# Cross-attention and a mixture-of-experts layer: operand rows spread over all partitions, one normalisation folded into the weights, raw operands kept apart, new orders

## What is computed

```python
h = x + xattn(layernorm(x), ctx, Wq, bq, Wk, bk, Wv, bv, Wo, bo)
out = h + ffn(layernorm(h), G, gate_w, up_w, down_w, lora_A, lora_B)

# xattn: 16 heads of 16
scores = jnp.einsum('bhsd,bhtd->bhst', Q, K) * scale
attn = jax.nn.softmax(scores, axis=-1)
ctx = jnp.einsum('bhst,bhtd->bhsd', attn, V)
# ffn: 8 experts, 2 of them weighted
scores = jax.nn.softmax(jnp.einsum('bsh,he->bse', x, G), axis=-1)
value, indices = jax.lax.top_k(scores, TOPK)
gate = jax.nn.silu(jnp.einsum('bsh,efh->bsef', x, gate_w))
up = jnp.einsum('bsh,efh->bsef', x, up_w)
out = jnp.einsum('bsef,bse,ehf->bsh', gate * up, w, down_w)
lr = jnp.einsum('bsh,erh->bser', x, lora_A)
out = out + LORA_SCALE * jnp.einsum('bser,bse,ehr->bsh', lr, w, lora_B)
```

## Time and profile before

| | us |
|---|---|
| median of 3 runs | 154.72 (154.31 to 155.24) |
| span of the profiled execution, first to last instruction | 150.3 |
| TensorE busy | 123.6 (82%) |
| VectorE busy | 93.0 (62%) |
| ScalarE busy | 68.7 (46%) |
| GpSimd busy | 49.3 (33%) |

### The profile page before, as it was taken

How to read it: one execution, slowest core, us unless ns; L and a number is a source line. 1 busy time by engine, 2 the same in 40 slices (tenths; PEclk the granted TensorE clock), 3 DMA queues, 4 the chain that set the end, 5 groups by cost and what they waited for, 6 DMA issues and landing times.

```text
span 150.3 us, 2628 instructions
## 1 busy us (share of the span) xinstructions
PE 123.6 (82%) x936; PEld 94.6 (63%) x936; DVE 93.0 (62%) x189; ACT 68.7 (46%) x116; POOL 49.3 (33%) x76
## 2 busy tenths in 40 slices
PE   5998661928998586499998499998999999999980
PEld 5996451928886463366574258755667578788760
DVE  4451606006498969238799569999859535866801
ACT  3116540241164243658937431989596731415110
POOL 7978602064052109800007030253500750250000
PEclk9999996595599879659999869999999999999999
DMA  4931699999999992000999100000000002002022
GB/s 133 258 133 38 144 128 187 122 156 134 171 240 142 146 255 40 2 4 4 156 122 124 20 0 4 0 4 2 7 0 0 0 4 70 0 0 74 0 74 70
DMA packets 9181, 11.92 MB, mean 79 GB/s; under 512 B 1296, under 2 KB 5712, under 8 KB 9168
## 3 DMA queue, kind: packets, MB, share of 16 engines
q1 hardware_dynamic: 8128, 10.56, 39.8%
q10 hardware_dynamic: 1040, 1.18, 4.6%
HBM read 4.34 MB, written 1.05 MB: 36 GB/s over the span
## 4 chain that ended last, share of the span: by engine, by line
PE 61%; DMA 13%; issue 7%; DVE 5%; SPq 4%; POOL 4%; ACT 3%; ACTq 0%; POOLq 0%; DVEq 0%
PE unit L719 23%; DMA qstack<-q_lo 8%; PE unit L832 7%; PE unit L800 7%; PE unit L726 5%; DMA kstack<-k_lo 5%; PE unit L819 5%; SPq L311 4%; PE unit L841 4%; PE unit L739 3%; PE unit L875 2%; POOL wf_lo L450 2%; PE unit L877 2%; PE unit L876 2%; DVE rowmax L644 1%
## 5 line engine op out<-in xcount | busy, mean ns | idle before, releaser
L644 DVE TENSOR_REDUCE rowmax<-unit 128x4 f32<-128x1024 f32 x32 | 37.7, 1214 | 18.6 <-PE unit L800 18.6
L549 ACT ACTIVATE probs<-unit 128x1024 f32<-128x1024 f32 x32 | 31.5, 1024 | 15.2 <-PE unit L819 9.8
L800 PE MATMUL unit<-kstack,qstack 48*128 48x256 f32 x128 | 16.0, 358 | 9.5 <-DMA qstack<-q_lo 3.3
L800 PEld LDWEIGHTS unit<-kstack,qstack 48*128 48x128 f32 x128 | 11.2, 227 | 15.7 <-issue 9.8
L426 POOL TENSOR_SCALAR vare<-mv 128x2 f32<-128x2 f32 x8 | 1.8, 223 | 52.2 <-DVE mv L591 52.1
L832 PE MATMUL unit<-probs,vaug 128*32 128x256 f32 x256 | 17.9, 409 | 0.0
L819 PE MATMUL unit<-qstack,kstack 49*128 49x256 f32 x128 | 13.7, 318 | 1.4 <-DVE rowmax L644 0.9
L819 PEld LDWEIGHTS unit<-qstack,kstack 49*128 49x128 f32 x128 | 10.1, 202 | 5.8 <-issue 2.9
L588 DVE BATCH_NORM_STATS2 stats<-xs 128x6 f32<-128x256 f32 x16 | 6.0, 418 | 9.9 <-DMA xs<-x 9.7
L832 PEld LDWEIGHTS unit<-probs,vaug 128*32 128x32 f32 x256 | 7.3, 115 | 6.3 <-issue 2.5
L719 PE MATMUL unit<-wf_hi,xT_hi 128*128 128x256 f32 (+1 forms) x32 | 9.4, 374 | 0.5 <-POOL xT_lo L441 0.5
(11 more groups left out here) (108 smaller groups left out, 241.6 us busy)
## 6 DMA issues: line engine op xcount, KB each, us to landing
kstack<-k_hi SPq DMA_DIRECT2D x16, 128.0 KB, 9.1
qstack<-q_hi SPq DMA_DIRECT2D x12, 128.0 KB, 8.2
xs<-x SPq DMA_DIRECT2D x4, 256.0 KB, 6.4
kstack<-k_lo SPq DMA_DIRECT2D x8, 128.0 KB, 10.8
out<-res SPq DMA_DIRECT2D x4, 256.0 KB, 2.2
probs<-wattn SPq DMA_DIRECT2D x3, 256.0 KB, 6.8
cT<-ctxT SPq DMA_DIRECT2D x3, 256.0 KB, 7.0
qstack<-q_lo SPq DMA_DIRECT2D x6, 128.0 KB, 7.0
```

The costliest lines, as they stand in the source:

```text
L549: act.activation(probs[:, n % NPAIR], unit[PAIR[name, n] // 2][:], ACT.Exp, scale=SCALE).then_inc(exp_done, 1)
L644: dve.tensor_reduce(rowmax[:, b % 2, :, :, i].rearrange("p t j -> p j t"), unit[PAIR[name, n] // 2][:], AX.X, ALU.max)\
L800: ins = pe.matmul(dst[:, j, t], qs[rows, i, t * P:(t + 1) * P], ks[rows, i], start=True, stop=True)
```

## The change

Six things change, and nearly every stage is written anew around them.

- **Rows of the stacks.** The part g of a stack now lies in the partitions g, g+4, g+8 and so on, 32 of them, and one transfer of 256 KB fills them from all 128 partitions of a part. A batch has six such transfers in place of twelve. The fourth row of each four, 3, 7, 11 and so on, is a filler: -1 in `kstack`, 0 in `qstack`, where the maxima then go into the partitions 63 and 127 with one transfer. The matmuls run over all 64 rows of a half. Fillers of stack 0 come from memsets, those of stacks 1 and 2 from four transfers of 256 KB (`fillk`, `fillq`) out of a small tile `edge`; batch 3 has a small one.
- **Raw operands.** `wk`, `wq`, `wv`, `wf` and all four contexts have tiles of their own. `probs` holds six pairs (four before).
- **Projections.** `k`, `q` and `v` of all batches are products of whole words. The splits of `wattn`, of the contexts and of the first transposes are gone (the new `wkh`, `chi` and their like stand in the code and in no order). `glu` stays of parts for batches 0 to 2 and is of whole words for batch 3; `low` is of whole words.
- **Second norm.** The weights of the second layer lose their column means once (`mean`, `mlow` on TensorE, `wfc`, `wlc` on VectorE). The rows go into the transpose as they are, and the reciprocal deviation is applied behind: as the scale of the tanh, in the routing and in the weights of the experts.
- **Smaller ones.** Ten warm-up matmuls (24 before). The tiles `xo`, `res` and `lw` are gone: the sums go back into `xs` and `low`. The ranks of the gates take four instructions in place of five.
- **Orders.** All five rows of `ORDERS` are new. SyncE issues all loads but those of ScalarE ahead of the first stack transfer, and all stack transfers.

The core of the diff:

```diff
-WHOLE = {("k", 0), ("q", 0), ("v", 0)}
+KV_PARTS = ()
+GLU_PARTS = (0, 1, 2)
+LOW_BY_VECTOR = (0,)
+NORM_BY_VECTOR = (0,)
...
     "sync": """
...
-        x:0 wv x:1 wk c:1 wq c:2 khi:0 x:2 c:3 klo:0 khi:1 qhi:1 x:3 klo:1 outs qlo:1 khi:2 qhi:2 wf klo:2
...
+        x:0 wk wv x:1 fillq:2 fillk:1 x:2 c:3 wo x:3 c:2 wd ks0:0 ks1:0 qs0:0 qs1:0 fillq:1 ks0:1 fillk:2 ks1:1
...
-        def stack_rows(engine, stack, parts, g, j, stacked):
-            lo = HALF * j + HD * g
-            engine.dma_start(stack[lo:lo + HD].bitcast(F32).rearrange("r (q k) t -> r q (k t)", k=KT),
-                             parts[HALF * j:HALF * (j + 1)].bitcast(F32).rearrange("p k t -> p (k t)")).then_inc(stacked, 16)
...
+        def part_rows(stack, g):
+            return stack[g:P:4].bitcast(F32).rearrange("i (q k) t -> i q (k t)", k=KT)
+
+        def parts_of(tile):
+            return tile.bitcast(F32).rearrange("p k t -> p (k t)")
...
+                    for g in (0, 1):
+                        sp.dma_start(part_rows(kstack[b], g), parts_of(k_hi[:, b % 2])).then_inc(k_stacked[b], 16)
...
+                        sp.dma_start(qstack[b][3:P:4].bitcast(F32),
+                                     edge[:, 1].bitcast(F32).unsqueeze(1).to_broadcast([QUAD, PAIRS, S]))\
+                            .then_inc(q_stacked[b], 16)
...
+                    wait_stacked(sp, "q", b)
+                    sp.dma_start(qstack[b][HALF - 1:P:HALF].bitcast(F32),
+                                 mT[:, b % 2].bitcast(F32)).then_inc(m_stacked[b], 16)
...
+                if name == "mean":
+                    wait(pe, "ones")
+                    pe.wait_ge(wf_in, 16)
+                    for k in range(KT):
+                        ins = pe.matmul(dst.rearrange("p o f -> p (o f)"), mean[:], wf[:, k, 0:2 * EF],
+                                        start=(k == 0), stop=(k == KT - 1))
```

More of the change, by code:

```diff
@@ L22 @@
 QUAD = 32
-GROUPS = HEADS // 4
 BLK = S // QUAD
@@ L42 @@
+GLU_PARTS = (0, 1, 2)
+LOW_BY_VECTOR = (0,)
+NORM_BY_VECTOR = (0,)
+WEIGHED_BY_GPSIMD = (0, 1, 2)
 ORDERS = {
     "tensor": """
[L44 to L56, removed]
+        xT:0@0 k:0@1 q:0@0 k:1@2 mean@1 xT:2@0 xT:1@3 bias@4 max:0.0@6 max:0.1@2 q:1@5 max:0.2@0 max:0.3@2 k:2@4
+        max:0.4@6 max:0.5@2 v:0@5 max:0.6@0 max:0.7@6 q:2@4 max:1.0@2 max:1.1@6 k:3@5 max:1.2@0 mrow:0@4 v:2@2
@@ L57 @@
     """,
     "scalar": """
[L59 to L63, removed]
+        c:0 wq biases obias c:1 wf xTE:0 khi:0 qhi:0 n1:1 n1:2 khi:1 kw:1 xTE:1 xTE:2 qhi:1 qw:1 n1:3 khi:2 kw:2
@@ new lines, in _ @@
+                if name == "wlc":
+                    wait(dve, "mlow")
+                    for k in range(KT):
+                        ins = dve.tensor_tensor(wf[:, k, 2 * EF:], wf[:, k, 2 * EF:], work[BANK["mlow", 0, 0]][:, 0, 0:LOW],
+                                                ALU.subtract)
+                    ins.then_inc(done["wlc"], 1)
+                if name == "mx":
+                    wait(dve, "max", b, i)
+                    if b >= 2 and i == 0:
+                        wait(dve, "mrow", b - 2)
+                    dve.tensor_reduce(rowmax[:, b % 2, :, :, i].rearrange("p t j -> p j t"), unit[BANK["max", b, i] // 2][:],
+                                      AX.X, ALU.max).then_inc(done["mx"], 1)
@@ L713, in _ @@
+                if name == "wl":
+                    weigh_low(dve, done, b)
+                if name == "wh":
+                    weigh_hidden(dve, done, b)
+                if name == "res":
+                    wait(dve, "down", b)
+                    dve.tensor_tensor(xs[:, b], work[BANK["down", b, 0]], xs[:, b], ALU.add).then_inc(done["res"], 1)
         @block.tensor
         def _(pe):
-            def product(dst, left, right, terms=((0, 0), (0, 1), (1, 0))):
+            done = raised["tensor"]
@@ L789, in _ @@
+                if name == "mlow":
+                    wait(pe, "ones")
+                    pe.wait_ge(wf_in, 16)
+                    for k in range(KT):
+                        ins = pe.matmul(dst[:, 0, 0:LOW], mean[:], wf[:, k, 2 * EF:], start=(k == 0), stop=(k == KT - 1))
+                    ins.then_inc(done["mlow"], 1)
                 if name == "max":
-                    n = PAIRS * b + i
                     if i == 0:
-                        wait_stacked(pe, k_stacked, b)
-                        wait_stacked(pe, q_stacked, b)
```

1101 lines of the change are left out of this document (543 added, 558 removed).

## The result

The changed kernel takes **128.68 us** (median, 128.62 to 128.92), beside 154.84 us (154.31 to 155.24) for the kernel before on the same chip: a ratio of 0.838, interval 0.831 to 0.845. The prediction said 142.0 us in a range of 134 to 153. Medians are over all executions, a ratio is over the undisturbed ones of both kernels, so the two can differ by up to a per cent.

What follows compares the result with a forecast made beforehand. Full DMA engines at half rate bound the early part, TensorE the part behind 85 us. Span: 26.3 + 100.8 + 3.1 + 3 + 4.4 = 137.6, plus 4.4 to the median: 142.0 us, range 134 to 153.

Steps and rivals of the forecast that it cites:

- The rate of the transfers: Stack transfers spread over all 128 partitions: taken at 250 GB/s, between 109 for narrow copies and 273 for loads.
- Up to the first `max`: Loads end at 17.9 us, then 2.1 MB of copies take 8.4 us: first `max` at 26.3, before 34.35.
- The bound at the other end: Earliest first `max`, 22.5 us: batch 3 of `x` lands at 17.4, then moments, `q_lo` on VectorE and its transfer.
- Cover of the warm-up: Start of the kernel: the lower clock left by fewer warm-up matmuls hides in the wait before the first `max`, costing nothing.
- TensorE's units: TensorE's work behind the first `max`, priced by the earlier trace's rows at full clock: 100.8 us.
- The same sum for the kernel before: Check from 62.02 to 146.64 us: units 77.9, clock 4.8 and idle 2.8 make 85.5 against 84.6.
- Lower clock: Behind the first `max`: after TensorE stands still some 8 us, the lower clock level costs 3.1 us.
- Interplay of VectorE and TensorE: Between first and last `max`, both engines nearly full: 3 us lost waiting for each other, bounds -1.2 and 12.
- Tail: End of the kernel: `hT` through ScalarE 0.7, `res` 0.69 and the store 3.0, together 4.4 us.
- From span to median: Median of the runs stood 4.4 us over the profiled span, taking the span of 137.6 to 142.0 us.
- the rival with copies at 273 or more: First `max` at 22.5 and nothing lost in the mix: 134 us; the faster range, 134 to 139, had 0.12.
- lockstep: Rival: VectorE and TensorE lose 12 us in place of 3: 151 us; 0.14 shared with slow copies that still gain.

## Why the prediction was 13.3 us too high

Point by point, by its own steps:

- **The rate of the transfers**: "I take 250". This is the step that failed first. The rows gave 109 and 273 as ends, and I held the faster one to be the most that a mixture could reach, because it was the fastest row. It was not a limit of the engines: copies and loads together ran at 391 to 394, and copies alone at 361. With it one row was misread: the share is 0.91 for the loads and 0.95 for the narrow copies, not 0.95 in both.
- **Up to the first `max`**: 26.3 predicted, 22.63 measured, 3.7 us. The bound at the other end, 22.5, with its path (batch 3 of `x`, moments, `q_lo`, transfer), is what happened, wait by wait. The choice between the two ends failed, not the working: by 22.63 us the DMA engines had moved 6.8 MB (299 GB/s on average), more than the 6.4 MB that were to hold the first `max` until 26.3.
- **Cover of the warm-up**: I costed the lower clock that the ten warm-up matmuls may leave at nothing, since it hides "in the same wait". The lower level also came behind that wait, for 1.7 us. That the ten matmuls are the cause is not shown, as two runs with ten of them did not have it there.
- **TensorE's units**: 100.8 predicted. TensorE's busy time of 99.0 us behind the first `max`, less some 1.7 at the lower level, is 97.3. `max` and `attn` came to 22.9 in place of 27.9: two behind each other take 0.67, and one behind the other kind 0.24, while I had priced each at the 0.43 that the earlier trace rows show for one that follows something else. Transposes came to 6.5 in place of 8.1 (0.44 for four, not 0.62). Against it stand projections of 17.1 in place of 15.6 (1.92 each behind a `max`), `u` of 15.9 in place of 14.9, `o` 0.4 more and small ones. In all 3.5 us less. The same sum for the kernel before did not show this: it came out only 0.9 too large, since two errors stood against each other. From 62.02 to 146.64 it had 82.7 of work (77.9 and 4.8 for the clock) and 2.8 of waiting; the trace has TensorE busy for 79.4 us and idle for 5.2. Small slips in the sum itself do not matter: its parts as written make 100.7, four `low` at 0.92 are 3.7, and what the comparison left over is 0.9 and not the 1.2 of the lower bound.
- **Lower clock**: 3.1 predicted, some 1.7 measured. The 3.1 were taken from a longer stop; right before the first `max` TensorE stood for 2.2 us and not for 8.
- **Interplay of VectorE and TensorE**: 3 predicted. TensorE was idle for 2.2 us between the first `max` and its last matmul, 0.9 of it the wait for `hT` that I had in the tail, so 1.3. Nearly all of that, 1.1, was waiting for ScalarE's exponentials (`probs`), and none for `rowmax`: the wait that I priced did not come.
- **Tail**: 4.4 predicted, 3.2 + 0.9 measured.
- **From span to median**: "The median of the runs stood 4.4 over the profiled span". The changed kernel's executions take 1.7 to 1.8 us more than their spans (128.92 against 127.1). Two of the kernel before took 153.0 with a span of 151.3, and 152.44 with one of 150.7. So 1.7 is the least that lies around the span. The other 2.7 of my 4.4 did not carry over. The profiled execution, with a span of 150.3, lay at the low end of that kernel's, and some of them take more around the span (155.41 with 151.9); how the 2.7 divides between the two is not shown.

3.7 + 3.5 + 1.4 + 1.7 + 0.3 + 2.7 = 13.3 us, in the order start, units, lower clock, interplay, tail, span to median. The cover of the warm-up is no term of its own in this sum, since what it cost is inside the lower clock that was measured. No single term is a third of it. The two largest are the steps that failed: the rate of 250 that set the start, and TensorE's short units priced where they stood in the old order. All terms erred on the same side, and the low end of the range, the rival with copies at 273 or more, kept the units and the 4.4 as they were.

What was right: that the narrow rows were the bound and not the bytes; that there would be one wait for a stack left and it would be the first; that the wait for `wf_lo` would go; that VectorE and TensorE would not fall into lockstep; that TensorE would be all but full from 45 us on (94.6% up to 60, then 100 up to 115); that with slow copies the change would be worth next to nothing (with the narrow rows it is worth 1.1%). Wrong beside the sizes: that the lower clock would hide in the wait, and whole words at 0.15 us more each. At 0.31, the nine of them behind the first `max` cost TensorE 2.8 us, so the change gives back there part of what it gains.

## What to carry to other kernels

When the DMA engines are at nine tenths and move a third of what another stretch moves, look at which partitions the transfers write before counting bytes: the same 1.05 MB took 2.9 us on rows 4 apart and 7.6 us on neighbouring ones. When such a bound is taken away, look for stops further down that go with it: here they were nearly half of what the spread gained (8.4 of 17.6 us of span). Price short TensorE units by how they stand in the new order, not by their mean in the old one. A transfer that is not due yet still costs its issue, some 0.6 us and more while the DMA engines are full, to all that stand behind it in the queue, and a split of an operand costs its place in the row of its engine: the versions that start earlier won or lost 1.5 to 3 us each mostly by such places.

## What the runs showed of the hardware

- Queued loads and copies together moved 391 to 399 GB/s; the fastest stretch of the earlier trace rows was 273. The Trainium skill, SBUF — State Buffer, section on the setup-cost knee, gives 224 GB/s for a transfer of 256 KiB by itself; queued, they ran well above that.
- 32 neighbouring rows take a copy no faster than 16 (137 and 135 GB/s, in the next round 133 and 128).
- More rows in the product show no cost: at full clock two `max` behind each other took 0.74 us on TensorE over 64 rows in the changed kernel and 0.74 over 48 rows with the narrow rows. (The means of a record, 306 and 341 ns, also hold the clock, 0.973 against 0.894.)
- A product of whole words, 8 records, costs 0.31 us more than one of parts, 12 records, at the same columns and the same place (1.92 and 1.61; for `glu`, 4 records and 6, 1.91 and 1.60).
- The lower clock can come back behind a later, short stop: after a wait of 2.2 us before the first `max` the granted clock from 22.5 to 30 us was 0.77, which cost 1.7 us. With a wait of 2.0 us it was 1.00 in another run with the same ten warm-up matmuls, so no number of matmuls and no length of the wait here tells when it comes.
